# Hyena, two mixtures and linear attention on one core: result scaling and turned copies moved to the end of their slots, second mixture weights by Tanh

## The chip, the cores and the metric

The kernel runs on one core of a Trainium2 chip. The metric is the device time of one execution, in microseconds (us). The kernel before takes 646.74 us, the median of 3 runs (646.6 to 649.38). The engines are PE (matmuls), DVE (vector), ACT (activations), POOL (GpSimd, which here also issues the indirect DMAs) and SP (which issues the plain loads and stores). Each has a queue of its own that it works off in order; semaphores tie them together.

## The reference, cut to what matters

Input x is 2 x 2048 tokens of 128 features, fp32. Two layers, each of the form "x + mixer(norm(x)) + mixture of experts(norm(x))".

```python
# layer 0: Hyena convolution (order 2) + 8 experts, 4 chosen, and a shared expert
xn = layernorm(x)
x = x + hyena(xn) + moe0(xn)
# layer 1: linear attention with 16 heads + 8 experts, 2 chosen
xn = layernorm(x)
q, k = elu(xn @ wq + bq) + 1, elu(xn @ wk + bk) + 1
attn = (q @ (k.T @ v)) / (q . sum(k) + 1e-6) @ wo + bo
gate_hidden = einsum('nh,erh->ner', xn, W_A)
scores = sqrt(sum(gate_hidden * gate_hidden, axis=-1))       # one per expert
topk_scores, topk_idx = top_k(scores, 2)
topk_w = softmax(topk_scores)                                # the two weights of a token
y = einsum('nef,ehf->neh', silu(gate_hidden @ W_B) * (xn @ W_up), W_down)
x = x + attn + sum over the two chosen experts of topk_w * y
```

With s1 >= s2 the two scores of a token, the weights are 1 / (1 + exp(s2 - s1)) and exp(s2 - s1) / (1 + exp(s2 - s1)).

## The kernel before, in words

The first part (up to about 300 us) normalises, projects and convolves by matrix DFTs. The rest is one loop over 90 slots (`SLOTS`), written out by hand for each engine: POOL from line 878, ACT from 1125, DVE from 1685, PE from 2154. In each slot every engine issues its steps in the order of that text; `due(slot, at)` and `odd_due(slot, at)` say which chunk or which batch of tokens a step works on in this slot. Slots 0 to 47 carry layer 0's experts, six slots for each of 8 chunks of 512 tokens (`gate0`, `up0_step`, `down0_step`, DVE's `product0`, POOL's weighting), and beside them, some slots behind, the residual, the second norm, keys, values, queries and the router of layer 1.

Layer 1's experts work on sorted rows. For each batch of 8 tiles (1024 tokens; four batches) PE and ACT make squared router products (`expert_gates`, `square`), DVE sums them (`norm_sum`), ranks the experts (`rank`, lines 1452 to 1475), PE counts, DVE gives each token its row (`slots`, 1477) and builds lists of blocks (`tables`, 1497, in four parts). POOL takes the square root of the two top scores and their difference (`root_of_norms`, 840); ACT takes Exp of it (line 1173, slots 31, 41, 53 and 63 by `EXP_AT`); DVE makes the two weights (`weigh`, 1675 to 1683, slots 32, 42, 54 and 63 by `WEIGH_AT`): the second weight goes to column D + 2 of each token's row in XNF, the first minus the second to column D + 3. POOL then scatters the rows, 128 at a time, to DRAM (line 858).

Pairs of blocks follow from slot 52 (`PAIR0`); pair i has its main work in slot 52 + i, 36 pairs in all. SP loads 2 x 128 rows into a ring of 5. For pair i:

- `turn_rows(i)` on PE transposes the rows (line 2075), `rows_hi(i)` on ACT (1087) and `rows_lo(i)` on DVE (1598) split them, all for pair i + 1 at the start of the slot.
- `gate_up(i)` on PE is six matmuls (lines 1762 to 1764), `silu_pair(i)` on ACT (1094), `product(i)` on DVE (1606), and `places_of(i)` on DVE (1615 to 1620) reads from the rows where the results go and with which weight.
- one slot later `turn_products(i)` on PE (2104) and `turned(i)` on ACT (1101), the copy of the transposed products.
- two slots later `down_rows(i)` on PE (2119), which waits for `turned(i)` and for the scaling of the pair before, and `result_rows(i)` on DVE (1628), which scales the results from PSUM with the weights; POOL scatters them (873).

In slots 52 to 67 other work lies in the same queues. ACT runs `key_features` and `query_exp` (lines 1077 to 1080 and 1123) at the end of slots 55 and 61, DVE `key_sum` and `query_features` (1666, 1673) in slots 56 and 62, `rank` in 60 and 61, `slots` in 54 and 63, `tables` in 55 to 57 and 64 to 67, attention steps from slot 64. In ACT's slot `turned` stands behind `silu_pair` and before these; in DVE's, `result_rows` stands behind `places_of` and before these. Which table ACT needs (`ACT_TABLE_LOAD`) isn't in the code: loads are put in front of an activation when the kernel is built.

## Time and profile before

| what | us |
|---|---|
| median of 3 runs | 646.74 (646.6 to 649.38) |
| the profiled execution, whole | 649.94 |
| its span | 648.1 |
| PE busy | 567.0 (87%) |
| PE weight load busy | 467.6 (72%) |
| DVE busy | 447.0 (69%) |
| ACT busy | 300.8 (46%) |
| POOL busy | 298.2 (46%) |
| mean granted TensorE clock | 0.973 of full |

Busy times are sums over the whole span; weight loads run beside the matmuls. In the slot loop the engines take turns in being late, so what one instruction is worth is read from the chain of waits and from the timelines of the slot in question. In the timelines a line begins with the start (us from the span's start) and the duration; a bracket at its end gives how long the engine was idle before it and what released it. "remote" is a release that the profile could not put to an engine or a known queue; "issue" is time in which the engine waited for nothing that the profile shows.

### The profile page before, as it was taken

The numbers are of one execution on the slowest core, as the hardware profiler recorded it, in microseconds if no ns is written. First come the engines' busy times: TensorE is split into PE (matmuls) and PEld (weight loads), VectorE is DVE, ScalarE is ACT, GpSimd is POOL, SyncE is SP. The second block draws the span as 40 slices with busy tenths as digits, with TensorE's granted clock in tenths as the row PEclk, the third lists the DMA queues.
The fourth block names the chain that finished last, engine by engine and source line by source line (L and its number), as shares of the span: only waits on it lengthen the run. The fifth ranks groups of instructions, "written<-read, shape, count | busy, mean of one in ns | idle before, by whom it ended". The sixth has DMA issues, their size and how long they took to land.

```text
span 648.1 us, 10568 instructions
## 1 busy us (share of the span) xinstructions
PE 567.0 (87%) x3218; PEld 467.6 (72%) x3218; DVE 447.0 (69%) x1199; ACT 300.8 (46%) x558; POOL 298.2 (46%) x268
## 2 busy tenths in 40 slices
PE   5899999989899998999999999986877877888870
PEld 2879985667687677888888878765665666777660
DVE  6858998729721992344659989987787685656673
ACT  4460247655424441344577657855835433334230
POOL 5610030006561563265334458768344755666661
PEclk9999999999999998999999999997999799999995
DMA  7350031400023502133222232122211232322626
GB/s 215 128 243 17 2 129 33 97 9 2 21 110 110 172 0 65 59 93 94 75 67 79 70 100 79 39 99 68 56 55 59 59 89 71 82 73 67 208 74 223
DMA packets 48381, 54.94 MB, mean 85 GB/s; under 512 B 7029, under 2 KB 40374, under 8 KB 47271
## 3 DMA queue, kind: packets, MB, share of 16 engines
q1 hardware_dynamic: 43542, 42.99, 21.2%
q0 software_dynamic: 4320, 8.99, 4.1%
q10 hardware_dynamic: 466, 2.31, 1.6%
q8 instruction: 28, 0.46, 0.3%
q14 instruction: 25, 0.20, 0.1%
HBM read 36.22 MB, written 15.94 MB: 80 GB/s over the span
## 4 chain that ended last, share of the span: by engine, by line
PE 30%; DVE 12%; issue 9%; ACT 6%; POOL 4%; another core or an unknown queue 4%; DMA 2%; SPq 1%; POOLq 0%; ACTq 0%; DVEq 0%
PE banks L1762 4%; PE banks L1764 4%; PE banks L1763 4%; PE banks L1968 3%; PE banks L1882 2%; PE banks L2119 2%; PE banks L1874 2%; POOL arena L888 1%; PE banks L2104 1%; PE banks L1895 1%; PE banks L1896 1%; DVE arena L1606 1%; DMA arena<-result_rows 1%; PE banks L2075 1%
## 5 line engine op out<-in xcount | busy, mean ns | idle before, releaser
L873 POOL DMA_INDIRECT result_rows<-arena x71 | 69.3, 975 | 38.8 <-PE banks L1764 16.6
L858 POOL DMA_INDIRECT expert_rows<-arena x64 | 63.6, 994 | 40.6 <-issue 14.6
L822 POOL TENSOR_TENSOR arena<-arena 128x512 f32<-128x512 f32 x32 | 40.8, 1275 | 86.2 <-DVE arena L1431 86.2
L888 POOL TENSOR_TENSOR arena<-arena 128x512 f32<-128x512 f32 x32 | 42.4, 1325 | 68.2 <-DVE arena L1585 68.1
L1585 DVE TENSOR_TENSOR arena<-banks,arena 128x512 f32<-128x512 f32 x48 | 33.0, 688 | 42.5 <-PE banks L1764 33.5
L1968 PEld LDWEIGHTS banks<-arena 128*128 128x128 f32 x384 | 48.8, 191 | 6.9 <-POOL arena L888 3.0
L1968 PE MATMUL banks<-arena 128*128 128x128 f32 x384 | 51.6, 277 | 1.9 <-DVE arena L1585 1.1
L1874 PE MATMUL banks<-arena 128*128 128x512 f32 x96 | 50.5, 608 | 2.4 <-DVE arena L1431 1.1
L1882 PEld LDWEIGHTS banks<-arena 128*128 128x128 f32 x256 | 33.0, 191 | 19.0 <-POOL arena L822 14.4
L2119 PE MATMUL banks<-arena 128*128 x284 | 39.6, 284 | 7.4 <-DVE arena L1628 4.0
L1087 ACT ACTIVATE rows_hi<-banks 128x256 fp32r<-128x256 f32 (+1 forms) x36 | 13.6, 379 | 67.7 <-remote 33.6
L1149 ACT ACTIVATE arena<-banks 128x512 f32<-128x512 f32 x48 | 28.7, 599 | 35.0 <-PE banks L1764 28.6
L980 ACT ACTIVATE arena<-banks 128x512 f32<-128x512 f32 x48 | 28.7, 597 | 32.5 <-PE banks L1850 32.5
L2119 PEld LDWEIGHTS banks<-arena 128*128 128x128 f32 x284 | 35.8, 197 | 9.0 <-issue 9.0
L1429 DVE TENSOR_TENSOR arena<-banks,arena 128x512 f32<-128x512 f32 x32 | 22.1, 692 | 23.7 <-PE banks L1874 22.1
L1882 PE MATMUL banks<-arena 128*128 128x128 f32 x256 | 34.4, 277 | 4.0 <-POOL arena L822 4.0
L1762 PE MATMUL banks<-gate_up_weights_hi,rows_hi 128*128 x71 | 32.3, 454 | 6.0 <-DVE arena L1606 4.6
L1009 ACT ACTIVATE arena<-banks 128x512 f32<-128x512 f32 x32 | 19.1, 597 | 39.4 <-PE banks L1882 39.4
L1438 DVE TENSOR_TENSOR arena<-banks,arena 128x512 f32<-128x512 f32 x16 | 11.1, 692 | 36.2 <-PE banks L1896 36.2
L1762 PE MATMUL banks<-projection_hi,xnt_hi 128*128 128x384 f32 (+1 forms) x92 | 33.4, 363 | 2.6 <-DVE xnt_lo L1247 2.6
L1606 DVE TENSOR_TENSOR arena<-banks,arena 128x512 f32<-128x512 f32 (+1 forms) x36 | 24.4, 677 | 11.8 <-ACT arena L1094 10.0
L1763 PE MATMUL banks<-projection_lo,xnt_hi 128*128 128x384 f32 (+1 forms) x92 | 31.9, 347 | 0.0
(281 smaller groups left out, 1628.7 us busy)
## 6 DMA issues: line engine op xcount, KB each, us to landing
arena<-expert_weights SPq DMA_DIRECT2D x64, 128.0 KB, 3.4
arena<-expert_rows SPq DMA_DIRECT2D x71, 66.0 KB
arena<-in_x SPq DMA_DIRECT2D x8, 512.0 KB, 6.8
arena<-result_rows SPq DMA_DIRECT2D x8, 512.0 KB
arena<-in_dft_f SPq DMA_DIRECT2D x1, 2048.0 KB, 9.6
normed_hi<-xnt_hi SPq DMA_DIRECT2D x1, 2048.0 KB, 6.4
normed_lo<-xnt_lo SPq DMA_DIRECT2D x1, 2048.0 KB, 10.9
arena<-in_dft_i SPq DMA_DIRECT2D x1, 2048.0 KB, 7.7
```

The costliest lines, as they stand in the source:

```text
L822: nc.gpsimd.tensor_tensor(out=T1[:, q % 3, :], in0=T1[:, q % 3, :], in1=T2[:, q % 2, :], op=ALU.add).then_inc(y_in, 1)
L858: pool.indirect_dma_start(out=xrows, out_offset=bass.IndirectOffsetOnAxis(ap=SLOT[:, k, t:t + 1], axis=0), in_=XNF[:, t, :], in_offset=Non ...
L873: pool.indirect_dma_start(out=yrows, out_offset=bass.IndirectOffsetOnAxis(ap=DEST[:, i, n:n + 1], axis=0), in_=YB[:, i % YBUFS, n, :], in_ ...
L888: nc.gpsimd.tensor_tensor(out=AM0[slot % 2], in0=AM0[slot % 2], in1=WB0[:, m, :], op=ALU.mult).then_inc(weighted, 1)
L1585: nc.vector.tensor_tensor(out=AM0[n % 2], in0=PS[1], in1=SG0, op=ALU.mult).then_inc(mult_done, 1)
L1606: nc.vector.tensor_tensor(out=AM1[:, i % 2, 0:n], in0=pair_banks(i)[:, 0:n, F1W:2 * F1W], in1=SG1[:, i % 2, 0:n], op=ALU.mult).then_inc(mu ...
L1762: mm(o, lh, rh, start=start, stop=False, skip_group_check=True)
L1763: mm(o, lh, rl, start=False, stop=False, skip_group_check=True)
L1874: mm(PS[2 + J % 2], TURNF, ZT[:, J % 2, :], start=True, stop=True).then_inc(d_mm, 1)
L1882: ins = mm(PS[6 + q % 2][:, P * n:P * (n + 1)], T1[:, q % 3, P * n:P * (n + 1)], TURNI, start=True, stop=True)
L1968: ins = mm(PS[2][:, D * t:D * (t + 1)], AM0[n % 2][:, P * t:P * (t + 1)], DW0[:, m, :], start=False, stop=(m == N0 - 1), skip_group_check= ...
L2119: ins = mm(PS[6][:, P * s:P * (s + 1)], AMT[:, i % 2, 2 * s + f, :], DN_FLAT[:, at], start=(f == 0), stop=(f == 1), skip_group_check=True)
```

## The change

Three edits. DVE's `result_rows(i - 2)` moves from behind `places_of(i)` to behind the tables, the last thing in the slot but for the combining of results. ACT's `turned(i - 1)` moves from behind `silu_pair(i)` to the end of the slot, behind keys' features, queries' Exp and the small activation. The small activation is Tanh with scale -0.5, read from the difference of the scores and written straight to column D + 3 (the first weight minus the second is tanh((s1 - s2) / 2)); `weigh` makes the second weight from it by one scaled add. In the slots where the moved steps have nothing behind them (most from slot 68 on), the order of instructions is as before.

```diff
--- before.py
+++ after.py
@@ -81,7 +81,7 @@
 COMP_AT = (1, 3, 5, 7)
 UP_HI_AT, UP_LO_AT = 3, 4
 WA_AT, WQKV_AT = 5, 7
-EXP_AT = (19, 17, 17, 15)
+TANH_AT = (19, 17, 17, 15)
 WEIGH_AT = (20, 18, 18, 15)
 ROOT_AT = (16, 16, 16, 14)
 ATT_B, ATT_A = 12, 14
@@ -289,7 +289,6 @@
         PAD = view(rY + 1920, 4, 4 + BT, 8)
         POS = view(rY + 2304, BT, 8)
         TMP1 = view(rY + 2368, GT, 8)
-        W1ST = view(rY + 2496, T)
         SLOTF = view(rY + 2592, 2, T)
         SLOT = view(rY + 2656, 2, T).bitcast(I32)
         BLOCK_EF = view(rY + 2720, 72)
@@ -300,7 +299,7 @@
         START_ROW, ROW_STEP, TAKEN = (view(m0 + 160 + 16 * n, 16) for n in range(3))
         LISTS = view(m0, 216)
         assert m0 + 216 <= rA and max(b - a for a, b in zip(LISTED, LISTED[1:])) <= 31
-        EXP2, SUM2 = view(rY + 2944, T), view(rY + 2976, T)
+        DIFF2 = view(rY + 2944, T)
         assert rY + 3008 <= rY + 3072
 
         rW = rF
@@ -388,7 +387,7 @@
         xnt_hi = sem("xnt_hi")
 
         rt_sub = sem("rt_sub")
-        rt_exp = sem("rt_exp")
+        rt_soft = sem("rt_soft")
         rt_w = sem("rt_w")
         rt_tr = sem("rt_tr")
         rt_out = sem("rt_out")
@@ -844,7 +843,7 @@
                 tops = TOPS[:, :, ts]
                 link(nc.gpsimd.tensor_tensor(out=tops, in0=tops,
                                              in1=HALF[:, 1, 0:1].unsqueeze(1).broadcast_to((P, 2, BT)), op=ALU.pow))
-                nc.gpsimd.tensor_tensor(out=EXP2[:, ts], in0=TOPS[:, 1, ts], in1=TOPS[:, 0, ts], op=ALU.subtract)\
+                nc.gpsimd.tensor_tensor(out=DIFF2[:, ts], in0=TOPS[:, 1, ts], in1=TOPS[:, 0, ts], op=ALU.subtract)\
                   .then_inc(root_in, 1)
 
             sent = [0]
@@ -965,7 +964,7 @@
 
             def router0_exp(n):
                 act.wait_ge(rt_sub, n + 1)
-                nc.scalar.activation(SCO, SCO, ACT.Exp).then_inc(rt_exp, 1)
+                nc.scalar.activation(SCO, SCO, ACT.Exp).then_inc(rt_soft, 1)
 
 
             router0_exp(0)
@@ -1159,18 +1158,18 @@
                         attention_copy(n)
                 if 0 <= i < NP:
                     silu_pair(i)
-                if 1 <= i <= NP:
-                    turned(i - 1)
                 c = due(slot, 13)
                 if c is not None:
                     key_features(2 * c)
                     key_features(2 * c + 1)
                     query_exp(c)
-                for bt, at in enumerate(EXP_AT):
+                for bt, at in enumerate(TANH_AT):
                     if odd_due(slot, at) == bt:
                         act.wait_ge(root_in, bt + 1)
-                        e = EXP2[:, BT * bt:BT * (bt + 1)]
-                        nc.scalar.activation(e, e, ACT.Exp).then_inc(rt_exp, 1)
+                        ts = slice(BT * bt, BT * (bt + 1))
+                        nc.scalar.activation(XNF[:, ts, D + 3], DIFF2[:, ts], ACT.Tanh, scale=-0.5).then_inc(rt_soft, 1)
+                if 1 <= i <= NP:
+                    turned(i - 1)
 
 
         @block.vector
@@ -1299,7 +1298,7 @@
                     nc.vector.tensor_tensor(out=sco, in0=log, in1=per_tile(red, NI), op=ALU.subtract)\
                       .then_inc(rt_sub, 1)
                 if step == 1:
-                    dve.wait_ge(rt_exp, n + 1)
+                    dve.wait_ge(rt_soft, n + 1)
                     link(normalise(wgt, sco, red, red2, None, NI))
                     link(nc.vector.tensor_scalar(out=cor, in0=wgt, scalar1=ROUTB, scalar2=None, op0=ALU.add))
                 if step == 2:
@@ -1675,12 +1674,9 @@
             def weigh(bt):
 
                 ts = slice(BT * bt, BT * (bt + 1))
-                first, second = W1ST[:, ts], XNF[:, ts, D + 2]
-                dve.wait_ge(rt_exp, 2 + bt + 1)
-                link(nc.vector.tensor_scalar(out=SUM2[:, ts], in0=EXP2[:, ts], scalar1=1.0, scalar2=None, op0=ALU.add))
-                link(nc.vector.reciprocal(first, SUM2[:, ts]))
-                link(nc.vector.tensor_tensor(out=second, in0=first, in1=EXP2[:, ts], op=ALU.mult))
-                nc.vector.tensor_tensor(out=XNF[:, ts, D + 3], in0=first, in1=second, op=ALU.subtract).then_inc(rt_w, 1)
+                dve.wait_ge(rt_soft, 2 + bt + 1)
+                nc.vector.tensor_scalar(out=XNF[:, ts, D + 2], in0=XNF[:, ts, D + 3], scalar1=-0.5, scalar2=0.5,
+                                        op0=ALU.mult, op1=ALU.add).then_inc(rt_w, 1)
 
             for slot in range(SLOTS):
                 i = slot - PAIR0
@@ -1708,8 +1704,6 @@
                 if 0 <= i < NP:
                     product(i)
                     places_of(i)
-                if 2 <= i < NP + 2:
-                    result_rows(i - 2)
                 c = due(slot, 14)
                 if c is not None:
                     key_sum(2 * c)
@@ -1737,6 +1731,8 @@
                     for part, at in enumerate(TABLE_AT[bt]):
                         if odd_due(slot, at) == bt:
                             tables(bt, part)
+                if 2 <= i < NP + 2:
+                    result_rows(i - 2)
                 if i >= BACK_AT:
                     for t in range(BACK_STEP * (i - BACK_AT), min(BACK_STEP * (i - BACK_AT + 1), GT), 2):
                         combine(0, t, 2)
```

## Rows read from the trace of the kernel before

**Rows 1.** The page's chain that ended last, shares of the span by engine.
```profile
PE 30%; DVE 12%; issue 9%; ACT 6%; POOL 4%; another core or an unknown queue 4%; DMA 2%; SPq 1%; POOLq 0%; ACTq 0%; DVEq 0%
```
**Rows 2.** Groups by line, ACT: line, operation, count, busy and mean, idle before.
```profile
L1173 ACT ACT_TABLE_LOAD x3 | 3.8, 1283 | 0.1
```
**Rows 3.** Timeline of ACT, slots 61 to 64.
```profile
496.79 0.60 ACT L1101 ACTIVATE arena<-banks 128x512 f32<-128x512 f32 x1 [3.68 <-remote]
...
503.02 0.60 ACT L1094 ACTIVATE arena<-banks 128x512 f32<-128x512 f32 x1
...
514.93 0.60 ACT L1094 ACTIVATE arena<-banks 128x512 f32<-128x512 f32 x1 [2.08 <-remote]
```
**Rows 4.** Timeline of DVE, slots 61 to 63.
```profile
498.41 0.42 DVE L1628 TENSOR_TENSOR arena<-banks,arena 128x256 f32<-128x256 f32 x1 [3.05 <-remote]
...
502.56 0.41 DVE L1598 TENSOR_TENSOR rows_lo<-banks,rows_hi 128x256 fp32r<-128x256 f32 x1
...
510.83 0.43 DVE L1628 TENSOR_TENSOR arena<-banks,arena 128x256 f32<-128x256 f32 x1 [1.46 <-PE banks L2119]
...
513.34 0.41 DVE L1680 TENSOR_SCALAR arena<-arena 128x8 f32<-128x8 f32 x1
```
**Rows 5.** Timeline of DVE, slot 32.
```profile
373.63 0.17 DVE L1680 TENSOR_SCALAR arena<-arena 128x8 f32<-128x8 f32 x1
...
374.39 0.69 DVE L1585 TENSOR_TENSOR arena<-banks,arena 128x512 f32<-128x512 f32 x1
```
**Rows 6.** Timeline of PE, slot 32.
```profile
375.14 0.50 PE L1762 MATMUL banks<-normed_chunk_hi,up_weights_hi 128*128 128x512 f32 x1 [0.44 <-DVE arena L1585]
```
**Rows 7.** Timeline of DVE, slot 42.
```profile
410.77 0.16 DVE L1680 TENSOR_SCALAR arena<-arena 128x8 f32<-128x8 f32 x1
...
411.52 0.69 DVE L1585 TENSOR_TENSOR arena<-banks,arena 128x512 f32<-128x512 f32 x1
```
**Rows 8.** Timeline of ACT, slots 41 and 42.
```profile
407.52 1.28 ACT L1173 ACT_TABLE_LOAD   x1
...
409.14 1.28 ACT L1149 ACT_TABLE_LOAD   x1
```
**Rows 9.** Timeline of ACT, slots 53 to 56.
```profile
454.68 1.28 ACT L1173 ACT_TABLE_LOAD   x1
...
462.11 0.60 ACT L1101 ACTIVATE arena<-banks 128x512 f32<-128x512 f32 x1 [0.38 <-PE banks L2104]
...
466.15 0.62 ACT L1123 ACTIVATE arena<-arena 128x512 f32<-128x512 f32 x1
...
468.83 0.60 ACT L1094 ACTIVATE arena<-banks 128x512 f32<-128x512 f32 x1
```
**Rows 10.** Timeline of DVE, slots 54 to 56.
```profile
456.49 0.42 DVE L1598 TENSOR_TENSOR rows_lo<-banks,rows_hi 128x256 fp32r<-128x256 f32 x1 [0.65 <-ACT rows_hi L1087]
...
458.40 0.69 DVE L1606 TENSOR_TENSOR arena<-banks,arena 128x512 f32<-128x512 f32 x1 [0.29 <-ACT arena L1094]
...
472.44 0.42 DVE L1628 TENSOR_TENSOR arena<-banks,arena 128x256 f32<-128x256 f32 x1 [1.68 <-remote]
472.78 0.75 DVE L1666 TENSOR_TENSOR arena<-arena 128x256 f32<-128x256 f32 x2
```
**Rows 11.** Timeline of PE, slot 57.
```profile
473.25 0.71 PE L2055 MATMUL banks<-arena 128*128 128x129 f32 x4 [1.29 <-DVE arena L1666]
```
**Rows 12.** Timeline of PE, slot 63.
```profile
504.49 0.79 PE L1762 MATMUL banks<-gate_up_weights_hi,rows_hi 128*128 x1 [0.95 <-DVE arena L1606]
```
**Rows 13.** Windows: PE, PEld, DVE, ACT, POOL busy, clock, DMA share, GB/s.
```profile
500.00:510.00 10.00, 6.79 (x29) 5.72 (x28) 7.16 (x29) 5.74 (x12) 6.39 (x5) 0.69 0.19 53
```
**Rows 14.** Timeline of DVE, slots 65 and 66.
```profile
523.13 0.42 DVE L1628 TENSOR_TENSOR arena<-banks,arena 128x256 f32<-128x256 f32 x1
...
526.29 0.41 DVE L1598 TENSOR_TENSOR rows_lo<-banks,rows_hi 128x256 fp32r<-128x256 f32 x1
```
**Rows 15.** Timeline of PE, slot 66.
```profile
524.95 1.06 PE L2119 MATMUL banks<-arena 128*128 x8
```

## The prediction

> **What bounds the kernel now.** I read the page's chain first [rows 1]: no engine holds it, so a local saving counts only where the chain passes at that moment. The changed lines are in the slot loop, so I then went through the timelines of ACT, DVE, PE and POOL slot by slot (Silu of pair i on ACT stands in slot 52 + i). The weights of the second mixture are made four times, and in three of them ACT loads a table for Exp [rows 2] and one more to go back to Silu. The reader is to see in the rows that in slots 32 and 42 DVE is the late engine, that from slot 53 to 58 the chain alternates between DVE and ACT, and that in slots 56, 61 and 63 DVE waits for PE's down product in front of work that doesn't need it.
>
> PE's records and its waiters don't always agree. In slot 61 the copy of turned products starts 3.68 us after ACT was free, and the scaling of results 3.05 us after DVE was [rows 3, 4], both released by "remote", although PE's own instructions stand earlier. Whatever holds these releases, nothing in this change removes it; it can only be worked under.
>
> **The weights (DVE).** Four small instructions become one. From the first to the product behind them is 373.63 to 374.39 = 0.76 us, one of them takes 0.17, so 0.59 is saved each time [rows 5]. In slot 32 PE waited 0.44 us for that product [rows 6] and DVE stays full behind it. Bounds 0 and 0.6; I take 0.5. In slot 42 the same block stands between the low part of the normed rows and the product, 410.77 to 411.52 [rows 7]; bounds 0 and 0.6, I take 0.5 again. In slots 54 and 63 their share is inside the terms below. No wait is added by the one scaled add, only its place moves.
>
> **The table loads (ACT).** The trace of before holds no Tanh. The two loads of slot 41 start 1.62 us apart with an Exp of 128x8 between them [rows 8], which leaves 0.3 for the Exp; that is the lower bound for a Tanh, the 0.60 of a 128x512 Silu [rows 3] the upper; I take 0.3, as for the same shape. Whether it needs loads isn't shown. At best none in slots 41, 53 and 63: 6 x 1.28 = 7.7 us less of ACT's time; in slot 31 the load only moves, since the queries' Exp stands before it. At worst all stay and slot 31 gets one more. I take the best case, with a chance for the other below. In slot 42 ACT's gain isn't on the path: DVE was busy until 411.52.
>
> By those two rows a switch costs the 1.28 us of the load and no more. The Trainium skill, ScalarE: Activation LUTs, section What ACT_TABLE_LOAD costs, adds a drain of about 1.38 us to each, 2.66 in all; this trace disagrees, and by that rule the six loads would be 16 us of ACT's time. The same page's section on table sets lists tanh with exp and with sigmoid, and silu with none of them; read strictly this speaks against the change, and it is the rival "loads stay" below.
>
> **Slots 53 and 54.** The load at 454.68 [rows 9] holds up the high copy of pair 3's rows, and DVE waited 0.65 us for it at 456.49; Silu of pair 2, behind the second load, held DVE's product another 0.29 at 458.40 [rows 10]. Both go: 0.9. Next late is DVE itself. The scaling of results then follows the places (2.1 us by slot 63 [rows 4]), the weights and a sum of squares, some 2.9 us later, and PE's down product of the next slot waits for it; so the 0.6 us of the weights in slot 54 I count as given back. Bounds 0 (PE waits for all of it) and 1.5; I take 0.9.
>
> **Slot 55.** ACT copied the turned products at 462.11, having waited 0.38 for PE, then ran the keys' features and the queries' Exp to 466.8 and came to Silu of pair 4 at 468.83 [rows 9]. Now the features start behind Silu of pair 3 and the copy follows them. The wait goes, the copy is only moved. Queued for the copy is PE's down product of slot 56, behind that slot's six gate and up matmuls, so a copy at about 465.5 is in time. Bounds 0 and 0.8; I take 0.4.
>
> **Slots 56 and 57.** DVE's scaling waited 1.68 us to 472.44, and only then came the keys' sums at 472.78 [rows 10], for which PE waited 1.29 us [rows 11]. Now the sums come first. DVE is full from there to slot 58, so its 1.68 us would be gained whole, but the scaling now stands behind a tables' step too, and PE waits for it. Bounds 0 and 1.7; I take 0.9. Slots 53 to 57 together: 0.9 + 0.4 + 0.9 = 2.2.
>
> **Slot 61.** The largest term. ACT waited 3.68 us to 496.79 with some 4.2 us of features behind the copy (slot 55 ran them from 462.6 to 466.8 [rows 9]), and came to Silu of pair 10 at 503.02 [rows 3]. DVE waited 3.05 us to 498.41 with the ranking of the last batch behind the scaling, 4.15 us up to the next low part at 502.56 [rows 4]. Now both waits are filled: the ranking ends at about 499.2, the features at 497.3, both engines come to slot 62 some 3 us earlier, and PE's gate and up product of slot 63 at 504.49 [rows 12] with them. If the delay falls elsewhere in the changed run, the features still don't wait for turned products: 0.4 as in slot 55. Bounds 0.4 and 3.05; I take 2.5, near the row. In those ten microseconds the granted clock was 0.69 [rows 13], so mostly the lower of its two levels (1.2 GHz), and PE had stood waiting for that product; a shorter wait may bring some back, which I don't count.
>
> **Slots 63 and 64.** DVE waited 1.46 us to 510.83 for the scaling, then made the places and from 513.34 the weights [rows 4]. Now both fill the wait: 1.46 + 0.6 = 2.1 us earlier. But Silu of pair 12, behind both loads, started at 514.93 after a "remote" wait of 2.08 [rows 3]. So bounds 0 and 2.1; near that row, 0.5. The scatter of the last batch is POOL's and waits for the gate product of slot 64 as well as for the weights; its 16 DMAs, and SP's loads behind them, shift with PE.
>
> **Sum.** 0.5 + 0.5 + 2.2 + 2.5 + 0.5 = 6.2 us. Against it I set 0.5 for PE's waits for the later scaling in slots 64 to 67, where DVE makes tables first. Net 5.7. The profiled execution took 649.94 us (span 648.1, 1.9 around it) and would come out at 644.2. It lay 3.2 us (0.5%) over the median; the forecast of the median is 646.74 - 5.7 = 641.0.
>
> **The rivals.**
> *Loads stay* (Tanh isn't held with Silu). No row shows the pair together. The 0.9 of slots 53 and 54 is lost, the rest is DVE's order: 641.9.
> *Waits refilled by PE.* The late releases fall in other places, or PE, which must wait for each later scaling, is late instead. Then only the small instructions count, 0.5 + 0.5, and some 0.8 of the rest: 644.9. For it: each DVE wait that is filled was itself a wait for PE. Against it: PE waited for DVE right behind two of them, in slots 57 and 63 [rows 11, 12].
> *Slower: scaling behind the tables.* In slot 65 the scaling was at 523.13 and the next slot's first instruction at 526.29 [rows 14], a part of the tables between them. At the slot's end it is about 2.8 us later, while PE's down product of slot 66 started at 524.95 [rows 15]: PE would wait 1.3 us, and with it the rows and gates of the next pair, queued behind. Slots 54, 57 and 64 are alike, at an estimated 1 us each. A PE idle that long can bring one more stretch at the lower level: 6.79 us of work at 0.69 [rows 13] would be 4.7 at full clock, so 2.1. 1.3 + 3.0 + 2.1 = 6.4, less the four small blocks' 2.4, is 4.0: 650.7. It decides where PE comes to its down product before the scaling ends and no attention step stops it right behind anyway; in slots 65 and 66 one does, which speaks against.
>
> **Chances.** Forecast 0.50 (own range 638.0 to 643.4), loads stay 0.15, refilled 0.23, slower 0.12. A measurement here tells about 0.5% (3.2 us) from no change. Faster by more: the first two and a little of the third, 0.66; within: 0.22; slower: 0.12. The upper bounds sum to 0.6 + 0.6 + 4.0 + 3.05 + 2.1 = 10.35, or 636.4, not likely all at once; the range is 637.5 to 646.4, reaching over the third case.
>
> **What would show it.** The three loads at the small activation gone, and their returns to Silu with them; one DVE instruction per batch of weights; the keys' features before the turned copy in slots 55 and 61; no wait of over 1 us on DVE in front of the keys' sums, the ranking and the places in slots 56, 61 and 63. It is wrong if PE's down products wait for DVE's scaling more than 3 us in sum longer than before, or if the time from slot 60 to slot 63 isn't shorter.

## The result, and the profile after

The changed kernel took 645.51 us (median of 20 runs, 639.85 to 650.17) where the kernel before took 649.12 beside it (20 runs, 643.94 to 655.74): ratio 0.994, interval 0.9917 to 0.9963, so about 3.9 us (2.4 to 5.4) instead of the 5.7 forecast. Measured again on two other chips it gave 0.9997 (0.996 to 1.0033) and 0.9896 (0.9849 to 0.9943). These two intervals don't touch: the gain depends on the chip, and how is the larger part of what follows. The profiled execution spans 643.9 us (before 648.1). Lines outside the edited steps are numbered 1 lower than before on POOL, ACT and DVE, 4 lower on PE. Its page, the busy line and the chain by engine (answers to [rows 1]):

```profile
PE 569.1 (88%) x3218; PEld 470.5 (73%) x3218; DVE 444.8 (69%) x1187; ACT 293.0 (46%) x552; POOL 299.1 (46%) x268
PE 29%; DVE 13%; issue 10%; ACT 5%; another core or an unknown queue 5%; POOL 3%; DMA 1%; SPq 0%; POOLq 0%; DVEq 0%; ACTq 0%
```

**The Tanh** is held together with Silu. ACT's table loads after, by line:

```profile
L1079 ACT ACT_TABLE_LOAD x8 | 10.3, 1283 | 0.0
L1148 ACT ACT_TABLE_LOAD x6 | 7.7, 1283 | 15.8 <-DVE arena L1437 15.7
L1093 ACT ACT_TABLE_LOAD x3 | 3.8, 1283 | 0.1
L1170 ACT ACTIVATE arena<-arena 128x8 f32<-128x8 f32 x4 | 0.9, 213 | 0.5 <-POOL arena L846 0.5
```

No load stands at the small activation any more [rows 2]; at the two Silus there were 7 and 5, now 6 and 3: six fewer in all, 7.7 us of ACT's time, and a Tanh of 128x8 takes 0.21 us. The Trainium skill, ScalarE: Activation LUTs, section on table sets, lists silu with none of the sets that it prints, so it couldn't decide this; the trace does.

**Slot 42.** DVE, then POOL, then PE, after:

```profile
412.67 0.17 DVE L1678 TENSOR_SCALAR arena<-arena 128x8 f32<-128x8 f32 x1
412.74 0.68 DVE L1584 TENSOR_TENSOR arena<-banks,arena 128x512 f32<-128x512 f32 x1
...
415.97 1.44 DVE L1193 TENSOR_SCALAR arena<-arena 128x4 f32<-128x4 f32 x1
```
```profile
412.55 0.99 POOL L857 DMA_INDIRECT expert_rows<-arena  x1 [0.17 <-issue]
413.84 0.96 POOL L857 DMA_INDIRECT expert_rows<-arena  x1 [0.30 <-issue]
415.11 0.96 POOL L857 DMA_INDIRECT expert_rows<-arena  x1 [0.30 <-issue]
416.09 1.29 POOL L887 TENSOR_TENSOR arena<-arena 128x512 f32<-128x512 f32 x1
```
```profile
417.43 1.16 PE L1964 MATMUL banks<-arena 128*128 128x128 f32 x8 [0.84 <-POOL arena L887]
```

The weights now end at once before the product [rows 7], but the product's reader on POOL, the weighting (L887), stands behind slot 41's last three scatters and starts without a wait, 2.7 us after the product ended. PE then waits 0.84 us for it.

**Slots 61 to 65.** ACT after (answers to [rows 3]), then DVE (to [rows 4, 14]), then PE:

```profile
490.75 0.60 ACT L1093 ACTIVATE arena<-banks 128x512 f32<-128x512 f32 x1 [0.29 <-PE banks L1760]
491.24 0.41 ACT L1076 ACTIVATE arena<-arena 128x256 f32<-128x256 f32 x1
...
495.31 0.58 ACT L1100 ACTIVATE arena<-banks 128x512 f32<-128x512 f32 x1
...
498.34 0.60 ACT L1093 ACTIVATE arena<-banks 128x512 f32<-128x512 f32 x1
...
506.98 0.60 ACT L1093 ACTIVATE arena<-banks 128x512 f32<-128x512 f32 x1 [2.71 <-remote]
514.16 0.60 ACT L1100 ACTIVATE arena<-banks 128x512 f32<-128x512 f32 x1 [6.58 <-remote]
```
```profile
497.19 0.22 DVE L1474 TENSOR_REDUCE arena<-arena 128x8 f32<-128x64 f32 x1
497.33 0.42 DVE L1627 TENSOR_TENSOR arena<-banks,arena 128x256 f32<-128x256 f32 x1
...
514.33 0.42 DVE L1627 TENSOR_TENSOR arena<-banks,arena 128x256 f32<-128x256 f32 x1 [3.48 <-remote]
```
```profile
498.00 1.15 PE L2115 MATMUL banks<-arena 128*128 x8 [1.35 <-DVE arena L1627]
...
505.51 0.60 PE L2100 MATMUL banks<-arena 128*128 128x128 f32 x4
...
514.90 1.09 PE L2100 MATMUL banks<-arena 128*128 128x128 f32 x4 [4.80 <-ACT arena L1100]
```

In slot 61 the moves did what the prediction said: features, then the copy with no wait before it; ranking, then the scaling with none. Silu of slot 62 comes at 498.34 instead of 503.02, though this trace had reached slot 30 2.6 us later than the trace before. But three slots later new "remote" waits stand: the copy of slot 64 waited 6.58 us for products whose four matmuls end on the record at 506.11, DVE 3.48 us, and PE then 4.80 us for the copy.

### The profile page after: what moved, and what is told of

Read it like the earlier page. It is cut to its first block, busy times and chain, and to the rows that moved or that the text cites. A ratio compares the mean times of both kernels' runs of the same rounds, so it can differ in the third digit from the quotient of the medians.

```text
span 643.9 us, 10548 instructions
## 1 busy us (share of the span) xinstructions
PE 569.1 (88%) x3218; PEld 470.5 (73%) x3218; DVE 444.8 (69%) x1187; ACT 293.0 (46%) x552; POOL 299.1 (46%) x268
## 3 DMA queue, kind: packets, MB, share of 16 engines
q10 hardware_dynamic: 466, 2.31, 1.7%
## 4 chain that ended last, share of the span: by engine, by line
PE 29%; DVE 13%; issue 10%; ACT 5%; another core or an unknown queue 5%; POOL 3%; DMA 1%; SPq 0%; POOLq 0%; DVEq 0%; ACTq 0%
PE banks L1758 4%; PE banks L1760 3%; PE banks L1759 3%; PE banks L1964 3%; PE banks L2115 2%; PE banks L1878 2%; DVE arena L1605 2%; PE banks L1870 2%; POOL arena L887 1%; PE banks L1891 1%; PE banks L1892 1%; PE banks L2071 1%; DMA arena<-result_rows 1%; PE banks L2100 1%
## 5 line engine op out<-in xcount | busy, mean ns | idle before, releaser
L857 POOL DMA_INDIRECT expert_rows<-arena x64 | 63.9, 998 | 37.6 <-issue 14.2
L887 POOL TENSOR_TENSOR arena<-arena 128x512 f32<-128x512 f32 x32 | 42.4, 1324 | 67.5 <-DVE arena L1584 67.4
L1964 PEld LDWEIGHTS banks<-arena 128*128 128x128 f32 x384 | 48.8, 191 | 7.6 <-POOL arena L887 3.5
L1878 PEld LDWEIGHTS banks<-arena 128*128 128x128 f32 x256 | 33.6, 194 | 19.0 <-POOL arena L821 14.4
L2115 PEld LDWEIGHTS banks<-arena 128*128 128x128 f32 x284 | 35.8, 197 | 15.5 <-issue 15.4
L1148 ACT ACTIVATE arena<-banks 128x512 f32<-128x512 f32 x48 | 28.7, 599 | 36.4 <-PE banks L1760 30.1
L1859 PEld LDWEIGHTS banks<-arena 128*128 128x128 f32 x192 | 22.9, 142 | 12.5 <-issue 8.5
```

Source lines behind the costliest of these rows:

```text
L857: pool.indirect_dma_start(out=xrows, out_offset=bass.IndirectOffsetOnAxis(ap=SLOT[:, k, t:t + 1], axis=0), in_=XNF[:, t, :], in_offset=Non ...
L887: nc.gpsimd.tensor_tensor(out=AM0[slot % 2], in0=AM0[slot % 2], in1=WB0[:, m, :], op=ALU.mult).then_inc(weighted, 1)
L1878: ins = mm(PS[6 + q % 2][:, P * n:P * (n + 1)], T1[:, q % 3, P * n:P * (n + 1)], TURNI, start=True, stop=True)
L1964: ins = mm(PS[2][:, D * t:D * (t + 1)], AM0[n % 2][:, P * t:P * (t + 1)], DW0[:, m, :], start=False, stop=(m == N0 - 1), skip_group_check= ...
L2115: ins = mm(PS[6][:, P * s:P * (s + 1)], AMT[:, i % 2, 2 * s + f, :], DN_FLAT[:, at], start=(f == 0), stop=(f == 1), skip_group_check=True)
```

## The experiments

Eighteen runs; the chips are numbered in the order in which they were used, and the result above is from chip 1. To compare traces I took the start of ACT's Silu in each slot (L1148 up to slot 47, L1093 from 52), set both traces to zero at slot 30, and subtracted the kernel before's first trace. Negative is earlier. "Third" and "again" are the changed kernel once more, on chips 5 and 4; the columns "Tanh again", "moves again" and "before again" are from chip 5 too.

| slot | after | third | again | Tanh only | Tanh again | moves only | moves again | rows only | turned only | before again |
|---|---|---|---|---|---|---|---|---|---|---|
| 34 | -0.68 | -0.68 | -0.68 | -0.67 | -0.69 | -0.01 | 0.00 | 0.00 | 0.00 | 0.01 |
| 43 | -1.30 | -1.30 | -1.28 | -1.28 | -1.29 | 0.00 | 0.00 | 0.79 | 0.01 | 0.74 |
| 44 | -0.70 | -0.69 | -0.70 | -0.69 | -0.69 | -0.02 | 0.00 | 0.78 | -0.02 | 0.74 |
| 53 | -2.06 | -1.41 | -2.08 | -1.41 | -0.27 | -0.04 | 0.01 | 0.05 | 1.00 | 0.64 |
| 54 | -3.35 | -2.68 | -3.36 | -2.69 | -1.57 | -0.29 | -0.24 | 0.06 | 0.74 | 0.64 |
| 57 | -4.60 | -3.93 | -4.62 | -2.85 | -1.73 | -1.93 | -2.03 | -0.83 | 0.74 | 0.69 |
| 60 | -4.34 | -4.91 | -5.58 | -2.83 | -1.67 | -1.80 | -2.98 | -0.97 | 0.75 | 0.69 |
| 62 | -7.27 | -4.31 | -8.65 | -2.10 | -0.13 | -4.52 | -2.39 | -3.26 | -2.10 | -0.68 |
| 64 | -10.55 | -4.93 | -11.26 | -2.83 | -1.60 | -3.58 | -1.44 | -3.59 | 0.59 | 0.49 |
| 66 | -5.89 | -4.89 | -11.62 | -2.92 | -0.22 | -4.46 | -2.31 | -2.31 | 0.43 | 0.46 |
| 87 | -6.53 | -4.05 | -20.76 | -2.35 | 2.95 | -2.05 | -2.17 | -3.81 | 1.85 | -0.24 |

The ratios to the kernel before on the same chip (12 executions each; 11 of pool_spread, 6 of rows_mid, after_third and mid_spread_again):

| run (chip) | us, before beside it | ratio (interval) |
|---|---|---|
| tanh_only (2) | 648.74, 652.74 | 0.9951 (0.9916 to 0.9986) |
| rows_only (2) | 650.91 | 0.998 (0.9945 to 1.0015) |
| turned_only (2) | 653.49 | 1.0031 (0.9996 to 1.0066) |
| moves_only (2) | 647.46 | 0.9907 (0.9872 to 0.9942) |
| after_shift96 (3) | 648.62, 652.46 | 0.9937 (0.9901 to 0.9973) |
| before_shift96 (3) | 653.19 | 0.9998 (0.9961 to 1.0035) |
| rows_mid (3) | 644.73 | 0.9896 (0.9845 to 0.9946) |
| pool_spread (3) | 646.06 | 0.991 (0.9875 to 0.9946) |
| after_again (4) | 629.23, 629.58 | 0.9997 (0.996 to 1.0033) |
| mid_spread (4) | 628.77 | 0.9959 (0.9918 to 1.0) |
| moves_mid (4) | 628.75 | 0.9971 (0.9934 to 1.0009) |
| tanh_mid (4) | 627.53 | 0.9957 (0.9917 to 0.9997) |
| before_again (5) | 653.79, 654.67 | 1.0003 (0.9963 to 1.0042) |
| after_third (5) | 647.78 | 0.9896 (0.9849 to 0.9943) |
| moves_again (5) | 651.5 | 0.9925 (0.9885 to 0.9966) |
| tanh_again (5) | 649.82 | 0.9948 (0.9914 to 0.9981) |
| mid_spread_again (6) | 642.9, 648.82 | 0.989 (0.9841 to 0.9939) |
| tanh_mid_again (6) | 646.32 | 0.9938 (0.9892 to 0.9984) |

**The change taken apart.** tanh_only is the changed kernel with both moves undone, moves_only the kernel before with both moves made, rows_only and turned_only with one:

```diff
-                if 2 <= i < NP + 2:          # behind places_of(i)
-                    result_rows(i - 2)
+                if 2 <= i < NP + 2:          # behind the tables: rows_only, moves_only
+                    result_rows(i - 2)
-                if 1 <= i <= NP:             # behind silu_pair(i)
-                    turned(i - 1)
+                if 1 <= i <= NP:             # end of ACT's slot: turned_only, moves_only
+                    turned(i - 1)
```

> Only the weights change: Tanh in place of Exp, one DVE instruction in place of four; the scaling of results and the turned copy stay where they were in the kernel before. Theory A (the moves carry the gain, the weights little): slot 32 comes out 0.7 us earlier against slot 30, slots 41 to 43 gain up to 1.3 us that is gone again by slot 44 because POOL's queue is full there, slot 54 gains 0.5 to 1.0, slot 64 gains at most 1; in all 1 to 2.5 us (0.15 to 0.4%). Rival B (the six table loads on ACT were the bound): 4 us or more, about the whole of the change's 0.6%.

> Only the scaling of results moves to the end of DVE's slot; the weights stay Exp, sum and reciprocal, the turned copy stays in front of the keys' features. Theory A: DVE's ranking in slot 61 and the keys' sums in slot 56 no longer wait for PE's down product, but ACT still runs the features of slots 55 and 61 behind the turned copy, so that Silu of the next pair comes late; gain 1 to 3 us. Rival B (DVE's waits were all of it): 4 us or more. Rival C (PE now waits for the later scaling in slots 54 to 67): no gain or a loss of up to 4 us.

> Only the turned copy moves to the end of ACT's slot. Theory A: ACT reaches Silu of pairs 4 and 10 earlier by 0.5 to 3 us, but DVE is still held by the scaling in slot 61, so that the product of pair 10 waits for DVE: gain 0 to 1.5 us. Rival B: ACT alone was late in slots 55 and 61, gain 3 us or more. Rival C: the copy comes too late for the down product of the next slot, loss of 1 us or more.

> Both moves, the weights as in the kernel before (Exp with its table loads, four DVE instructions). Theory A: most of the change's gain, 2.5 to 4.5 us, since slots 55 to 62 are untouched by the weights; slot 63 loses against the changed kernel because the Exp and its two loads now stand in front of the turned copy of pair 10. Rival B (the loads were the bound): no more than 1.5 us.

Slots 34, 43 and 44 belong to the weights alone, the same to 0.02 us in the five Tanh columns. (rows_only and before_again stand 0.74 to 0.79 us late there, with nothing edited in these slots: a single trace can be off by that much.) From slot 53 to 54 every kernel with Tanh and the old or new order gains 1.27 to 1.30, those with the old weights 0 to 0.26: that is the loads, for this batch's weights are made on DVE only behind that Silu. From 54 to 57 the moves bring 1.64 and 1.79, Tanh 0.16. By medians each single move is worth nothing that can be told (-0.2%, +0.3%), both together 0.9%. With one move made, the engine of the other still waits in slot 61, which may be why. DVE and ACT there, in turned_only, tanh_only and rows_only, one fence each:

```profile
498.08 0.42 DVE L1628 TENSOR_TENSOR arena<-banks,arena 128x256 f32<-128x256 f32 x1 [3.08 <-remote]
```
```profile
494.38 0.60 ACT L1100 ACTIVATE arena<-banks 128x512 f32<-128x512 f32 x1 [4.42 <-remote]
...
495.28 0.43 DVE L1627 TENSOR_TENSOR arena<-banks,arena 128x256 f32<-128x256 f32 x1 [3.06 <-remote]
```
```profile
493.28 0.60 ACT L1094 ACTIVATE arena<-banks 128x512 f32<-128x512 f32 x1 [1.46 <-remote]
```

It isn't shown: in rows_only that wait is short, and its trace kept a lead of 3.26 us at slot 62 and 3.81 at slot 87, which the median of its runs doesn't show.

Against the expectations: tanh_only came out better than theory A (0.49% where it had up to 0.4%), and its interval of 0.14 to 0.84% takes in rival B's 4 us (0.61%) as well. moves_only gave 5.3 us between the medians, above theory A's 2.5 to 4.5. For rows_only and turned_only the intervals (0.55% faster to 0.15% slower, 0.04% faster to 0.66% slower) leave both theory A and rival C standing.

Tanh 0.5% and moves 0.9% don't add up to the change's 0.6%; with intervals of 0.35% each way that is not far outside them, and on chip 5 the same three gave 0.5, 0.75 and 1.0%.

**Does the late release (the "remote" one) follow PE's code?** 96 waits that are already met stand ahead of PE's slot loop, so that the transfers of PE's code come at other instructions:

```diff
+            for _ in range(96):
+                pe.wait_ge(fill_set, 3)
             for slot in range(SLOTS):
```

> The changed kernel with 96 waits put in front of PE's slot loop, on a semaphore that has long reached its value: the work is the same, PE's instructions lie 96 places later in its code. In the traces so far the releases that PE gives come 2 to 7 us late in stretches that begin shortly after a 16384-byte transfer of instructions (at 489.6 and 511.8 us in the kernel before, 485.8 and 507.2 in the changed one), always at the same place of PE's program. Theory A (the late stretches belong to the blocks of PE's code): the transfers come one to two slots earlier in the program and the late stretches of slots 61 and 64 move with them; the stall of about 5 us in slot 65 goes or moves to slots 62 to 63, and the whole moves by -3 to +3 us. Rival B (the stretches belong to the work, its DMAs or the row loads): the transfers move, the late stretches stay in slots 61 and 64, the time stays within 0.5 us of the changed kernel.

> The kernel before with the same 96 waits on PE. Theory A: its late stretches move by the same number of instructions as in the changed kernel, the wait of the scaling in slot 61 (3.05 us) and that of the turned copy (3.68 us) are gone or much shorter, and slots 61 to 63 come 2 us or more earlier against slot 60 than in the kernel before; part of what the changed kernel gained there would then have been the cover of this stall. Rival B: slot 61 keeps its waits of over 3 us.

The code transfers near slot 61 moved from 489.6 and 511.8 to 486.8 and 509.2 us, while before_shift96 kept every slot from 30 to 61 within 0.05 us of the kernel before, and its waits of slot 61 stayed:

```profile
498.29 0.60 ACT L1101 ACTIVATE arena<-banks 128x512 f32<-128x512 f32 x1 [4.46 <-remote]
```
```profile
499.18 0.42 DVE L1628 TENSOR_TENSOR arena<-banks,arena 128x256 f32<-128x256 f32 x1 [3.09 <-remote]
```

So the two waits of slot 61 don't follow the code's transfers; for the later ones it isn't shown. From slot 71 its trace is 4 to 6 us behind, at a ratio of 0.9998: one pair of traces says little about the late slots. after_shift96 by itself looked like theory A: ACT waited 4.50 us for the copy at the end of slot 60, and the stall of slot 65 was gone. But after_third, below, has both without a shift, so this run parts nothing.

**Order and scatters.** rows_mid is the change with the scaling ahead of the tables but behind ranking and sums; pool_spread is the change with slot 41's scatters spread over later slots:

```diff
+                if 2 <= i < NP + 2:
+                    result_rows(i - 2)
                 for bt in range(NBT):
                     for part, at in enumerate(TABLE_AT[bt]):
```
```diff
-SCATTERS = ((1, 3, 3, 1, 1, 2, 1, 1, 3), (1, 1, 1, 3, 3, 2, 2, 2, 1))
+SCATTERS = ((1, 3, 3, 1, 1, 2, 1, 1, 1, 2), (1, 1, 1, 3, 3, 2, 2, 2, 1))
```

> The changed kernel with the scaling of results between the ranking and the tables, in place of behind the tables. Theory A (PE's waits for the scaling behind the tables cost part of the gain, the changed kernel shows 8.8 us of PE idle for it against 4.0): slots 56 to 58 and 65 to 68 come 0.5 to 2 us earlier, the wait of PE for line 1627 falls by 2 us or more. Rival B (these waits are hidden, since the attention steps and the next product wait for DVE anyway): the same within 0.5 us.

> The changed kernel with two of the three scatters that POOL issues in slot 41 moved behind the weighting of slot 42. Theory A (the 1.3 us that slots 42 and 43 gain are gone by slot 44 because POOL's weighting stands behind scatters without a gap): slot 44 and 47 come 0.6 to 1.3 us earlier against slot 30 than in the changed kernel, 1.3 to 2.0 earlier than in the kernel before. Rival B (DVE, whose small instruction for the variance then lasts 1.44 us beside POOL's, or PE is the bound of slot 43 anyway): slot 44 stays at -0.7.

pool_spread shows the cause of slot 42's loss: slot 44 at -1.78 in place of -0.70, slot 47 at -1.40 in place of -0.70, as its theory A had it. POOL there weighs the product between two scatters, and DVE's small add, which now runs ahead of the weighting, is short:

```profile
413.72 0.96 POOL L857 DMA_INDIRECT expert_rows<-arena  x1 [0.30 <-issue]
414.70 1.32 POOL L887 TENSOR_TENSOR arena<-arena 128x512 f32<-128x512 f32 x1
```
```profile
413.36 0.17 DVE L1193 TENSOR_SCALAR arena<-arena 128x4 f32<-128x4 f32 x1
```

In the changed kernel that same add of 128x4 took 1.44 us and ended with POOL's 1.29 us weighting (415.97 to 417.41, 416.09 to 417.38); in the kernel before it took 0.76 us and ended with the weighting too (415.51, 415.47). The Trainium skill, SBUF — State Buffer, section SBUF: two separate sides, has DVE, in some of its instructions, and GpSimd arbitrate for one port pair that whoever has it keeps for a whole instruction. The trace agrees in that the add ends with POOL's instruction; its record begins 0.12 us before the weighting, while the last scatter still runs (415.11 to 416.07), and which instruction held the ports when isn't shown. Nor did the spread show in the time beyond doubt: 0.991 (0.9875 to 0.9946) beside 0.9937 of after_shift96 on the same chip.

rows_mid's theory A wasn't borne out. PE's wait for line 1627 fell to 8.2 us, not by 2 or more, and from slot 53 to 57 it gained 2.55 us, like the changed kernel. Its 0.9896 rests on 6 runs, and its interval overlaps the change's; what made it better, if it is, isn't shown.

**The change once more, and the order again.** moves_mid is rows_mid with the old weights, mid_spread has rows_mid's order and the spread, tanh_mid rows_mid's order with the copies where they were.

> The changed kernel once more, nothing edited: how much of what its first trace showed comes again. Theory A (the stall of slot 65 is what the two moves make of the order: PE idle 4.8 us for a turned copy that waited 6.6 us) expects that stall of over 4 us again, slot 64's lead of about -10.5 us and its fall to about -6 by slot 66. Theory B (slots 33 to 44 are fixed by the order, while from slot 52 on the late releases of PE fall where they will, so that one profile differs from the next by 2 to 4 us) expects slots 33, 42 and 44 at -0.35, -1.97 and -0.70 within 0.03, the lead at slot 64 between -3 and -11 and at the end between -3 and -8. Both: a ratio to the kernel before of 0.993 to 0.996.

> The change with both orders that the runs before pointed to: results scaled before the tables (but behind the ranking and the sums), and slot 41's row scatters spread so that slot 42's weighting isn't behind three of them. If the two gains add: slots 44 and 47 at -1.78 and -1.40 as in the spread kernel, PE's waits for the scaling at about 7 us, and a ratio to the kernel before of 0.985 to 0.989. If the spread's 0.7 us is lost in the later slots, as the gain of slot 42 was: 0.989 to 0.991, no different from the same kernel without the spread.

> The kernel before with its own weights (Exp, sum, reciprocal), the turned copies last on ACT and the results scaled behind the ranking but ahead of the tables. Theory A (the moves bring the gain of slots 61 to 63, the Tanh some 1.3 us at slot 54 and 0.6 us in slot 32 beside it, and the sum is what is measured): 0.991 to 0.993, that is some 2 us behind the same order with Tanh. Theory B (Tanh adds nothing once the moves are made, as the change's 0.994 beside the moves' 0.991 may mean): the same 0.989 to 0.991 as with Tanh. In both slots 33 to 47 at 0 and no -1.3 at slot 54 but for the moves' own.

> Tanh and the results scaled behind the ranking and ahead of the tables; the turned copies stay behind Silu. It tells whether the copies' move is worth anything: the features in slots 55 and 61 again stand behind a copy that waits for PE. If the copy's wait binds ACT in slot 61 (some 3 us before Silu of slot 62): slot 62 at no more than -3 and a ratio of 0.993 to 0.996, some 2 us behind the kernel with both moves. If DVE's order alone is what counts: slot 62 at -5 to -6 and 0.989 to 0.991.

This chip behaved otherwise than the rest. The kernel before took 629.58 us there, 3.0 to 3.8% less than on the other five, and in none of the four traces is there one "remote" release in the waits' table; in the first two traces there are 33.6 + 14.5 + 10.3 = 58 us of them before ACT's row copies, DVE's scaling and ACT's turned copies, and 27.3 + 11.4 + 8.9 = 48 after. The chain of after_again has no unknown queue, and PE's group of down products waits longer for the scaling:

```profile
PE 32%; DVE 12%; issue 8%; POOL 6%; ACT 5%; DMA 3%; SPq 0%; POOLq 0%; DVEq 0%; ACTq 0%
L2115 PE MATMUL banks<-arena 128*128 x284 | 40.3, 287 | 12.6 <-DVE arena L1627 12.2
```

against, in the first trace after and the first trace before:

```profile
L2115 PE MATMUL banks<-arena 128*128 x284 | 40.4, 286 | 12.5 <-DVE arena L1627 8.8
```
```profile
L2119 PE MATMUL banks<-arena 128*128 x284 | 39.6, 284 | 7.4 <-DVE arena L1628 4.0
```

Up to slot 58 after_again keeps the first trace's shifts to 0.02 us (-4.94 in both); from slot 60 on they part, and at slot 66 it is 5.7 us ahead, at slot 87 14.2. The stretch 550 to 580 us, then 580 to 610, of the first trace and of after_again (columns as in [rows 13]):

```profile
550.00:580.00 30.00, 24.69 (x169) 20.99 (x167) 17.71 (x67) 11.06 (x23) 18.46 (x20) 1.00 0.26 75
580.00:610.00 30.00, 25.60 (x168) 21.62 (x169) 18.97 (x74) 9.58 (x20) 19.07 (x20) 0.98 0.46 146
```
```profile
550.00:580.00 30.00, 29.68 (x215) 26.70 (x214) 21.98 (x83) 12.93 (x27) 21.94 (x23) 1.00 0.30 87
580.00:610.00 30.00, 27.12 (x193) 23.83 (x191) 24.74 (x89) 11.56 (x23) 21.90 (x24) 1.00 0.47 157
```

More work per microsecond, and the granted clock is 1.00 in both first windows: in this stretch it isn't the clock. Nor is the wait of slot 61 there. The copy of tanh_mid stands where it stood before the change and starts without a wait; in after_again PE waits for the moved one:

```profile
488.42 0.62 ACT L1100 ACTIVATE arena<-banks 128x512 f32<-128x512 f32 x1
```
```profile
493.06 0.63 PE L2100 MATMUL banks<-arena 128*128 128x128 f32 x4 [1.67 <-ACT arena L1100]
```

The stall of slot 65 (4.80 us) isn't there either, nor in after_third below, so theory A of after_again, that the two moves make it, fell. Theory B had slots 33, 42 and 44 right (-0.35, -1.96, -0.70) and the late part wrong (-11.26 at slot 64, -20.76 at slot 87). The ratios of after_again, mid_spread and moves_mid came out nearer to 1 than any range given for them, for the ranges had been taken from chips with late releases; tanh_mid's 0.9957 lies in its first range, but with slot 62 at -9.02 in place of -3.

**Before and after side by side again.** The two kernels and the two halves of the change, unedited.

> The kernel before, for its trace on the chip of this call. On the last chip four kernels took about 629 us, and their four traces had none of the stretches from 430 us on in which what waits for PE starts 2 to 7 us behind PE's record. Theory A (ACT's 3.68 and DVE's 3.05 us in slot 61, which the moves fill, are such stretches, a state of the chip and not of the code): on a chip with stretches the two waits are there and a run takes 647 to 653 us; on one without, both waits of slot 61 are under 1 us and a run takes about 630. Theory B (the waits come of the order of the code, and the last chip was only quicker elsewhere): both waits over 2 us on either.

> The changed kernel a third time, nothing edited, beside before_again on one chip. Theory A: where the stretches are, the ratio to the kernel before is 0.992 to 0.996; where they are not, 0.997 to 1.001, because the waits that the moved steps fill aren't there, while PE's waits for the later scaling (12.2 us on the last chip, 8.8 on the first) are. Theory B: 0.992 to 0.996 on either.

> Both moves with the old weights, again. Theory A: with stretches 0.989 to 0.994 as the first time; without them 1.001 to 1.004, since the moves then bring PE's longer waits for the scaling alone. Theory B: 0.989 to 0.994 on either.

> The new weights alone, again. Both theories: 0.994 to 0.998 on either kind of chip, for the 0.68 us of slot 32 and the 1.3 us of slot 54 hang on no late release. Under theory A it is without stretches the better part of the change, and at least as good as the whole of it.

This chip (654.67 us for the kernel before) has the late releases. Slot 61 of before_again, ACT and DVE:

```profile
495.62 0.60 ACT L1101 ACTIVATE arena<-banks 128x512 f32<-128x512 f32 x1 [2.31 <-remote]
```
```profile
498.62 0.42 DVE L1628 TENSOR_TENSOR arena<-banks,arena 128x256 f32<-128x256 f32 x1 [3.04 <-remote]
```

and the change is worth 1.0%, the moves 0.75%, Tanh 0.5%. For a chip with late releases theories A and B expected the same, so these runs don't part them. What speaks for A is the quick chip alone: no late release in four traces, and 0.9997. The kernel before was not traced there. PE's waits for the scaling were 4.8 us in after_third and 4.7 in before_again, so the 4.8 us by which they grew in the first pair of traces didn't come again.

after_third also shows what stood in place of the wait of slot 61. At the end of slot 60 ACT stood still for the copy:

```profile
489.79 0.60 ACT L1100 ACTIVATE arena<-banks 128x512 f32<-128x512 f32 x1 [5.02 <-remote]
```

Six traces on chips with late releases have both moves with the scaling behind the tables, and four of them have such a wait there (moves_again 5.02, after_shift96 4.50, pool_spread 4.48 us). Against before_again, on the same chip, after_third stood at -5.60 us at slot 60 and at -5.42 at slot 64: its lead came before slot 61, and slots 61 to 63 added nothing.

**The best order once more.** mid_spread and tanh_mid, unedited.

> The change with the results scaled behind the ranking but ahead of the tables, and slot 41's scatters spread, a second time. On a chip with the stretches of late releases both theories of its gain are tested: if the moves' 0.7 to 0.9% of those chips, the Tanh's 0.5% and the order's share add, 0.984 to 0.989; if they fill the same waits, 0.988 to 0.993, no more than the change itself has there. Without stretches 0.995 to 0.998, as the first time.

> Tanh and the results' order alone (turned copies where they were), a second time. With the stretches: ACT's wait for the copy in slot 61 is there again with the features behind it, so slot 62 at -2 to -3 and 0.993 to 0.996, behind mid_spread_again. If it matches mid_spread_again, the copies' move is worth nothing on such a chip either. Without stretches 0.995 to 0.998.

mid_spread_again came out at 0.989 (6 runs), the edge of both its ranges, which decides nothing; tanh_mid_again at 0.9938. For the second I had expected slot 62 at -2 to -3; it was -7.59, with a wait of 0.79 us before the copy of slot 61. Once the scaling stands behind the ranking, the copy's place isn't what counts in that slot. The two ratios' intervals overlap, and what the copies' move is worth stays open. mid_spread has 0.989 and 0.9959 on the two kinds of chip, where the change has 0.9896 to 0.994 and 0.9997. It beats the kernel before on the first kind; that it beats the change too isn't settled, for the intervals overlap.

## Why the prediction was wrong

The forecast was 641.0 with a range of 637.5 to 646.4; 645.51 came. Of the 4.5 us, 2.4 are the starting point: the three runs shown had a median of 646.74, twenty had 649.12. The other 2.1 are the gain, 3.6 us between the medians in place of 5.7.

**Slot 32:** 0.5 forecast, 0.67 to 0.69 in the traces with Tanh. Right.

**Slot 42:** 0.5 forecast. Slots 42 and 43 started 1.3 and 0.6 us earlier than slot 41 had, and slot 44 gave it back. I looked at DVE and ACT and not at POOL's queue, through which the product goes to PE. Wrong, and shown by pool_spread.

**Slots 53 to 57:** 2.2 forecast (0.9 + 0.4 + 0.9); between slots 53 and 57 the changed kernel gained 2.54, 2.52 and 2.54, of it 1.28 by the loads and 1.25 behind. Right, the loads a little low, and "loads stay" refuted. But part of the 1.25 is again a wait marked remote, DVE's 1.68 us of slot 56 [rows 10].

**Slot 61, the largest term, 2.5, and slots 63 and 64, 0.5:** from slot 60 to 63 the three traces of the changed kernel (chips 1, 5 and 4) gained 4.2, 0.7 and 1.9 us on the first trace before, to slot 64 6.2, 0.0 and 5.7; the last compares two kinds of chip. In the first the mechanism is as described, and at slot 64 the sum stood at 10.55 us. Then one late release of 6.58 us took 4.7 of it by slot 66. The prediction saw "Whatever holds these releases, nothing in this change removes it; it can only be worked under", and then counted 2.5 us for working under it, as if the wait stood still while the work around it moved. This is the step that failed. By slot 58 the first trace stood at -4.94 us, and after_third at -4.95 against before_again, where the forecast had 0.5 + 0.5 + 2.2 = 3.2; the medians of chip 1 leave 3.6 at the end, so the 3.0 of slots 61 to 64 brought nothing that lasted there. What is filled in one slot can stand again in another: 6.58 us in slot 64 of the first trace, 4.48 to 5.02 us at the end of slot 60 in four others. On a chip without late releases there may be nothing to fill. What holds a release, and so why it stands again, stays open.

**PE's later waits, 0.5:** 8.8 - 4.0 = 4.8 us more in the first trace, 0.1 more on chip 5, and 12.2 in all on chip 4. The sign by which I had called the forecast wrong, more than 3 us of longer waits, came true in the first trace. What it cost the end isn't separated: rows_mid had 8.2 us and a ratio at least as good.

**The rivals.** "Waits refilled by PE" (644.9) is nearest in the absolute figure only because of the starting point; in gain it had 1.8 us, and the 3.9 measured lie between it and the forecast's 5.7. In mechanism it is the nearest, as far as it said that the late releases fall elsewhere. "Slower: scaling behind the tables" didn't come on any chip; with late releases that order (moves_only) gave 0.7 to 0.9%. On chip 4 the gain that was in place by slot 58 (if the kernel before runs there as elsewhere up to that slot, which wasn't traced and is doubtful, for its first trace has remote waits in slots 47 and 56) is gone at the end, and the kernels with the scaling ahead of the tables are 0.3 to 0.4% ahead of the kernel before; that fits, with overlapping intervals, and no more.

## What to carry to other kernels

Take a gain from a wait only if its releaser is known and stays where it is: a wait marked as remote, or as an unknown queue in the chain, is a property of this execution and chip until a second trace shows it again. Follow a value that is ready earlier through every queue to its reader, the one that only issues DMAs too. A gain that is the same to 0.02 us in every trace comes from the edit; one that differs by 3 us between traces of one kernel needs medians, on more than one chip.

## What the runs showed of the hardware

Five of the six chips on which the kernel before was timed gave 648.8 to 654.7 us, one 629.6, same kernel. The four traces of the quick one have no remote releases. The sixteen others have them, in slots where PE's record had ended up to 8 us earlier (506.11 and 514.16 us in the first trace after). In fifteen the first stands at 440 to 449 us, in slot 47, in the first trace after at 496.6. DVE's wait of slot 61 was 3.04 to 3.13 us in the six of them that have the scaling ahead of the ranking, and in the three of the sixteen with the scaling between ranking and tables (rows_mid, mid_spread_again, tanh_mid_again) no remote wait of over 1.5 us stands in slots 60 to 62. So the code has a part in where they fall, and, as far as one quick chip can tell, the chip in whether they do. What holds them was not found. That the waits of slot 61 follow PE's code transfers is excluded by the shift; the granted clock was 1.00 both with and without them from 550 to 580 us; DMA traffic wasn't tried.
